# A graph network on one core: transposed edge attributes made where they are used, and two engines' turns put in another order

## The chip, the cores and the metric

The kernel runs on one core of one Trainium2 chip. Its time is device microseconds, from the start of the program to its end. The kernel before took 1757.79 us (median of 3 runs, 1755.62 to 1760.14). A core has a matrix engine (TensorE, PE in the profile; PEld is its weight load), a vector engine (VectorE, DVE), a scalar engine (ScalarE, ACT), GpSimd (POOL) and SyncE (SP), which here only starts transfers. Each works through its own list of instructions in order and waits on semaphores for the others.

## The reference

`x` has 50000 nodes of 128 floats; there are 12500 edges (`src`, `dst`, sorted by `dst`) with attributes of 128 floats. A GraphSAGE part of two layers is followed by a graph transformer of four heads, each with a residual and a layer norm:

```python
x = _layernorm(x + _L0_gnn_ref(x, src, dst, ...))   # two layers: h @ W_self + mean of neighbours @ W_neigh + b
x = _layernorm(x + _L1_gnn_ref(x, edge_index, edge_attr_128, ...))
# inside _L1_gnn_ref, H = 4 heads of D = 128:
q, k, v = x @ Wq + bq, x @ Wk + bk, x @ Wv + bv
e = edge_attr @ We + be
alpha = einsum('ehd,ehd->eh', q[dst], k[src] + e) / sqrt(D)
attn = exp(alpha - amax[dst]) / denom[dst]            # softmax over the edges of one destination
agg = segment_sum((v[src] + e) * attn, dst)
out = agg + x @ Wskip + bskip
lin = (layernorm(out) * ln_g + ln_b) @ Wlin + blin
return elu(lin + x)
```

## The kernel before

Only rows that are the destination of an edge need the graph work. So the program first computes all 50000 rows as if they had no edge, and then does the edges again and scatters the rows that have some over the output. It has five stages with a barrier of all engines between them:

- setup (weights, index rows);
- stage b (`b_*`): all nodes, in 104 turns of 512 rows;
- stage a (`a_*`): first SAGE layer of the edges' rows;
- stage c (`c_*`): second SAGE layer for 12500 edges, in 25 turns of 512 edges (R = 4 tiles of 128). Beside that it reads the edge attributes, transposes them with TensorE (`c_pea`), copies them from PSUM with ScalarE (`c_eT`, line 1123), multiplies them by `We` (line 1108) and stores the product `ve_tab`. It also stores the transposed attributes in `eT_tab` (SyncE, line 1199);
- stage d (`d_*`): attention, layer norms and the scatter of the results, in 111 turns for 98 tiles of 128 edges.

Stage d is a software pipeline. In turn `it` four tiles are in work: `a` = it (gathered rows of source and destination transposed, line 1366; logits), `b` = it - 10 (values and the sum over the edges of one destination), `c` = it - 11 (first layer norm and product with `Wlin`) and `d` = it - 12 (elu, second layer norm, output). Once in 7 tiles a group of logits goes through a softmax by rows: transposed by TensorE, two scans (maxima), then two scans (sums), then a reciprocal, in three successive turns of VectorE. The order of the work on each engine is the order of the code in `d_pe`, `d_act`, `d_dve`, `d_pool` and `d_sync`; nothing reorders it. The steps of one turn that matter here:

- TensorE: 1366 transposes of source and destination rows (`d_pT`), 1373 and 1375 products with `Wv` and `Wskip` for tile b, 1386 with `Aqk` for tile a, 1392 four transposes of tile c (`d_pO`), 1397 with `Aqe` (`d_pP`: the logits' matrix in bank PB is complete), 1402 sum over the edges (`d_pN`), 1408 four products with `Wg` (`d_pY`).
- ScalarE: 1443 copy of the transposes (`d_xT`), 1449 first norm (`d_on`), 1455 exp, 1461 copy of shares (one turn in 7), 1468 values scaled by shares (`d_vex`), 1473 and 1475 the second norm's root (`d_rs2`), 1480 copy of tile c's transposes (`d_onT`), 1494 output (`d_o2`), 1499 and 1501 the first norm's root for tile b (`d_rs`).
- VectorE: 1592 residual (`d_z`), 1596 matrix of equal destinations (`d_same`), 1602 `d_nm`, 1608 values plus attributes (`d_vs`), 1612 and 1616 elu and residual, 1618 and 1622 statistics of the second norm (`d_bn2`), the group's scans (1555 to 1582) in three turns of 7, 1634 `d_nm2`, 1640 four logits (`d_al`), 1646 and 1650 statistics of the first norm (`d_s1`, `d_bn`).
- GpSimd: two gathers (1307), an addition (1320), the scatter of finished rows (1324).
- SyncE: transposed attributes of tile it + 3 read from `eT_tab` (1256), `ve_tab` rows (1260), four small stores of tile c (1266 to 1270).

In the code `after(eng, name, j)` makes the engine wait until step `name` is done for tile `j`.

Of the kernel before, what the change touches and what calls it, by code (L numbers as in the profile page):

```python
# [40 lines left out]
def gnn_kernel(nc, x, src, dst, edge_attr, Ws0, Wn0, b0, Ws1, Wn1, b1, Wq, bq, Wk, bk, Wv, bv, We, be,  # L41
# [21 lines left out]
    eT_tab = nc.dram_tensor("eT_tab", [NT * P, D], F32).ap()  # L63
# [4 lines left out]
    with ExitStack() as ctx:  # L68
# [99 lines left out]
        carve_at[0] = 0  # L168
        d_x1s = [carve(D) for _ in range(4)]
# [104 lines left out]

        def dma_et(k):
            return step(f"dma_et{k}")
# [833 lines left out]
        def c_act(act):  # L1110
            for s in range(NG + 2):
                if s < NG:
                    n = min(R, NT - R * s) * P
                    after(act, "c_pmT", s)
                    after(act, "c_py", s - 2)
                    after(act, "c_col", s - 2)
                    act.activation(c_mnT[s % 2][:, 0:n], MT[s % 2][:, 0:n], ACT.Copy).then_inc(step("c_mnT"), 1)
                    if s == LAST:
                        split_act(act, "c", tile_of(MT[s % 2], NT % R), c_mnT[s % 2][:])
                    after(act, "c_pea", s)  # L1120
                    after(act, "c_pve1", (R * s) // 2 - 1)
                    landed_before(act, dma_et(s % 2), s // 2)
                    act.activation(c_eT[s % 2][:].rearrange("p r d -> p (r d)")[:, 0:n], TE[:, 0:n],
                                   ACT.Copy).then_inc(step("c_eT"), 1)
                if s >= 2:
                    j = s - 2
                    after(act, "c_bn", j)
                    act.activation(a_st[:, 32:36], mv(a_st[:, 24:32])[:, :, 1], ACT.Ln, bias=eps[:, 0:1]).then_inc(step("c_l"), 1)
                    after(act, "c_l", j)
                    after(act, "c_n0", j - 1)  # L1130
                    act.activation(a_st[:, 36:40], a_st[:, 32:36], ACT.Exp, scale=-0.5).then_inc(step("c_r"), 1)
                    after(act, "c_nm", j)
                    landed_before(act, dma_cr[j % 2], j // 2)
                    for r in range(R):
                        t = act.activation(a_rows[j % 2][:, r, :], ypart[:, R * j + r, :], ACT.Identity,
                                           scale=a_st[:, 36 + r:37 + r], bias=a_st[:, 40 + r:41 + r])
                    t.then_inc(step("c_x1"), 1)
                if s < NG:
                    for r in tiles_of(s)[0::2]:
                        attr_out(act, lambda o, i: act.activation(o, i, ACT.Copy), s, r)  # L1140
# [40 lines left out]
        def c_sync(sp):  # L1181
            def load(s):
                after(sp, "c_pea", s - 2)
                if (s + 1) * BLK <= E:
                    sp.dma_start(c_ea[s % 2][:], edge_attr[s * BLK:(s + 1) * BLK, :].rearrange("(r p) d -> p r d", p=P)
# [9 lines left out]
            for s in range(NG + 2):  # L1195
                if s < NG:
                    n = len(tiles_of(s))
                    after(sp, "c_eT", s)
                    sp.dma_start(eT_tab[s * BLK:s * BLK + n * P, :].rearrange("(r p) d -> p r d", p=P),
                                 c_eT[s % 2][:, 0:n, :]).then_inc(dma_et(s % 2), 16)  # L1200
                    if s + 2 < NG:
                        load(s + 2)
# [5 lines left out]
                if s < NG:  # L1208
                    for r in tiles_of(s):
                        i = R * s + r  # L1210
                        after(sp, f"c_ve{r % 2}", i // 2)
                        sp.dma_start(ve_tab[i * P:(i + 1) * P, :], c_ve[i % 4][:]).then_inc(dma_vs(i % 4), 16)
            for k in range(2):
                sp.wait_ge(dma_cr[k], 16 * len(range(k, NG, 2)))
                sp.wait_ge(dma_et(k), 16 * len(range(k, NG, 2)))
# [37 lines left out]
        def d_sync(sp):  # L1253
            def load(j):
                after(sp, "d_pP", j - 4)
                sp.dma_start(d_xT[j % XT][:, 2 * D:3 * D], eT_tab[j * P:(j + 1) * P, :]).then_inc(dma_ea[j % 4], 16)
# [84 lines left out]
        def d_pe(pe):  # L1341
# [12 lines left out]
            for it in range(D_TURNS):  # L1354
# [6 lines left out]
                if live(a):  # L1361
                    pe.wait_ge(dma_xs[a % 4], 16 * (a // 4 + 1))
                    pe.wait_ge(dma_xd[a % 4], 16 * (a // 4 + 1))
                    after(pe, "d_xT", a - 1)
                    for i, s_ in enumerate((d_x1s[a % 4], d_x1d[a % XD])):
# [29 lines left out]
                if live(a):  # L1395
                    pe.wait_ge(dma_ea[a % 4], 16 * (a // 4 + 1))
# [39 lines left out]
        def d_act(act):  # L1436
            for it in range(D_TURNS):
                a, b, c, d = it, it - LAG, it - LAG - 1, it - LAG - 2

                if live(a):  # L1440
                    after(act, "d_pT", a)
                    after(act, "d_pN", a - XT)
                    act.activation(d_xT[a % XT][:, 0:2 * P], TB[:, 0:2 * P], ACT.Copy).then_inc(step("d_xT"), 1)
# [26 lines left out]

                if live(d):
# [4 lines left out]

                if live(c):
                    after(act, "d_pO", c)
                    after(act, "d_pY", c - 1)
                    act.activation(d_onT, OTB[:], ACT.Copy).then_inc(step("d_onT"), 1)  # L1480
# [41 lines left out]
            act.activation(f_out, f_sum, ACT.Identity, scale=f_rs2, bias=f_nm2).then_inc(step("f_out"), 1)  # L1522

        def d_dve(v):
# [59 lines left out]
            for it in range(D_TURNS):  # L1584
# [45 lines left out]

                if live(d):
# [5 lines left out]
                if live(a):  # L1637
                    after(v, "d_pP", a)
                    for h in range(H):
                        t = v.tensor_tensor_reduce(hs(d_junk, h), hs(PB, h), d_x1d[a % XD], SCALE, zero[:, 0:1],  # L1640
                                                   ALU.mult, ALU.add, d_al[:, H * a + h:H * a + h + 1])
# [124 lines left out]
```

## Time and profile before

| | us |
|---|---|
| median of 3 runs | 1757.79 |
| the profiled execution | 1751.26 |
| its span (first to last instruction) | 1749.4 |
| stage b | about 16 to 680 |
| stage a | about 680 to 847 |
| stage c | 847.6 (first load) to 1043 |
| stage d, first turns | 1043 to 1100 |
| stage d, full turns | 1100 to 1640 |
| stage d, last turns and end | 1640 to 1749.4 |

Over 1100 to 1640 us TensorE is busy for 525.3 of 540 us, VectorE for 406.3, ScalarE for 365.1 and GpSimd for 292.1. In stage c (847 to 1043 us, 196 us) they are busy for 153.2, 113.9, 105.3 and 97.9 us, and the DMA engines work at 0.75 of their time. How to read it: a matrix engine that is busy for 97% can still be waited for less than that says, because the ends of matmuls are modelled and a matmul row covers time in which the next one has already begun. What sets the length of a turn is read from a timeline: go from an instruction back to what it started right behind, until the same instruction of the turn before is reached. In each row of the timeline the first number is the start, the second the duration, and a bracket at the end says how long the engine had been idle and for whom.

### The profile page before, as it was taken

Reading aid. Unit: us, or ns where it says so; the run is one execution under the profiler, and the core shown is the slowest. Engines: PE = TensorE matmul, PEld = TensorE weight load, DVE = VectorE, ACT = ScalarE, POOL = GpSimd, SP = SyncE. Lnnn points to the kernel's source line nnn. Section 1 sums busy time; section 2 is a strip of 40 time slices with the busy share of each in tenths; the row PEclk is TensorE's granted clock in tenths of the full one; section 3 lists DMA queues with packets and bytes.
Section 4 is the critical chain, followed back from the end, with each engine's and each line's share of the span. In section 5 each row is a group of like instructions: output and inputs, shape, how many; then the busy total and the mean of one; then the engine's idle time right before and its main releaser. Section 6 shows DMA issues by size and latency. Waiting matters only on the chain. (4 is left out here: it accounts for less than half of the span.)

```text
span 1749.4 us, 34139 instructions
## 1 busy us (share of the span) xinstructions
PE 1524.3 (87%) x7745; PEld 1024.5 (59%) x7745; DVE 1327.1 (76%) x6197; ACT 1160.0 (66%) x3125; POOL 1041.2 (60%) x1038
## 2 busy tenths in 40 slices
PE   3599999999999998999688867999999999999872
PEld 2477777777777776777455543555555555455441
DVE  4799999999999996656366653777777777777762
ACT  0499999999999995333255541666666666666662
POOL 4688888868888773664455526455555555555320
PEclk9899999999999999999899988999999999999995
DMA  2356566544444442332388853233222232333210
GB/s 79 109 152 158 153 160 154 151 154 144 149 142 148 139 146 74 85 84 70 116 268 271 273 173 80 78 84 85 83 84 84 84 85 79 82 83 85 59 36 4
DMA packets 178820, 206.77 MB, mean 118 GB/s; under 512 B 36607, under 2 KB 104666, under 8 KB 178703
## 3 DMA queue, kind: packets, MB, share of 16 engines
q1 hardware_dynamic: 151502, 169.25, 31.5%
q0 software_dynamic: 27200, 36.26, 9.0%
q8 instruction: 37, 0.61, 0.2%
q14 instruction: 81, 0.66, 0.1%
HBM read 107.47 MB, written 106.49 MB: 122 GB/s over the span
## 5 line engine op out<-in xcount | busy, mean ns | idle before, releaser
L1307 POOL DMA_INDIRECT big<-x_tab,look x196 | 199.6, 1019 | 97.6 <-issue 56.1
L1324 POOL DMA_INDIRECT out_dram<-big,idx x98 | 99.2, 1013 | 259.1 <-DVE big L1640 126.3
L700 PE MATMUL pb<-MG_s,big 128*128 128x256 f32 x832 | 207.4, 392 | 41.5 <-issue 30.7
L700 PEld LDWEIGHTS pb<-MG_s,big 128*128 128x128 f32 x832 | 149.5, 189 | 143.7 <-issue 95.2
L725 ACT ACTIVATE big<-big 128x128 f32<-128x128 f32 x416 | 170.0, 481 | 0.0
L820 POOL TENSOR_TENSOR big<-big,cl 128x512 f32<-128x512 f32 x104 | 133.3, 1282 | 49.8 <-ACT big L749 40.5
L682 PE MATMUL pb<-C_s,big 128*128 128x128 f32 x832 | 161.6, 276 | 0.0
L683 PE MATMUL pb<-Ws1c_s,big 128*128 128x128 f32 x832 | 161.3, 276 | 0.0
L1057 POOL DMA_INDIRECT big<-h1e_tab,hidx x98 | 97.9, 999 | 103.9 <-PE pb L937 45.0
L334 POOL DMA_INDIRECT a_xs<-in_x_dram,idx x98 | 102.3, 1044 | 86.7 <-issue 47.6
L1408 PEld LDWEIGHTS pb<-Wg_s,big 128*128 128x128 f32 x784 | 95.8, 192 | 98.1 <-ACT big L1480 95.8
L860 POOL DMA_INDIRECT look<-redirect,idx x98 | 118.4, 1208 | 29.5 <-issue 29.2
L1640 DVE CUSTOM_DVE_ANT_0 big<-pb,big,zero 128x128 f32<-128x128 f32 x392 | 113.2, 342 | 28.2 <-PE pb L1397 25.9
L834 POOL DMA_INDIRECT redirect<-idx x98 | 112.3, 1146 | 30.9 <-issue 30.6
L1408 PE MATMUL pb<-Wg_s,big 128*128 128x128 f32 x784 | 114.2, 289 | 18.9 <-ACT big L1480 15.7
L683 PEld LDWEIGHTS pb<-Ws1c_s,big 128*128 128x128 f32 x832 | 126.9, 193 | 0.0
L682 PEld LDWEIGHTS pb<-C_s,big 128*128 128x128 f32 x832 | 126.9, 193 | 0.0
L749 ACT ACTIVATE big<-pb,big 128x128 f32<-128x128 f32 x416 | 118.9, 369 | 11.9
L716 ACT ACTIVATE big<-pb,vcol 128x512 f32<-128x512 f32 x104 | 71.5, 688 | 78.1 <-issue 59.1
L762 DVE CUSTOM_DVE_ANT_0 big<-pb,big,zero 128x128 f32<-128x128 f32 x416 | 120.5, 345 | 1.9 <-ACTq L256 1.9
L1108 PE MATMUL pb<-We_s,a_xs 128*128 128x512 f32 x196 | 99.3, 632 | 22.7 <-issue 19.0
L799 DVE SCALAR_TENSOR_TENSOR big<-pb,big 128x128 f32<-128x128 f32 x416 | 116.7, 343 | 1.4 <-issue 1.4
(345 smaller groups left out, 4015.1 us busy)
## 6 DMA issues: line engine op xcount, KB each, us to landing
big<-in_x_dram SPq DMA_DIRECT2D x104, 256.0 KB
x_tab<-big SPq DMA_DIRECT2D x98, 256.0 KB
out_dram<-big SPq DMA_DIRECT2D x98, 256.0 KB
ve_tab<-c_ve SPq DMA_DIRECT2D x98, 256.0 KB
c_ve<-ve_tab SPq DMA_DIRECT2D x98, 256.0 KB
h1e_tab<-a_rows SPq DMA_DIRECT2D x25, 256.0 KB
x_tab<-a_rows SPq DMA_DIRECT2D x25, 256.0 KB
big<-eT_tab SPq DMA_DIRECT2D x98, 64.0 KB
```

The lines of the kernel that those rows point to most:

```text
L682: pe.matmul(o, b_xT[(u - 1) % 2][:, r * P:(r + 1) * P], C_s[:], start=True, stop=False)
L683: t = pe.matmul(o, b_h1T[:, r * P:(r + 1) * P], Ws1c_s[:], start=False, stop=True)
L700: t = pe.matmul(o, b_x1T[:, r * P:(r + 1) * P], MG_s[:], start=True, stop=True)
L725: t = act.activation(b_o[u % 2][:, r * D:(r + 1) * D], b_w[u % 2][:, r * D:(r + 1) * D], ACT.Identity, scale=brs3[:, r:r + 1], bias=b_nm3[ ...
L749: t = act.activation(b_x1[(u - 1) % 4][:, r * D:(r + 1) * D], PY[(u - 1) % 2][:, r * D:(r + 1) * D], ACT.Copy, bias=1.0, scale=brs1[:, r:r ...
L762: t = v.tensor_tensor_reduce(b_junk[:, r * D:(r + 1) * D], PMG[(u - 3) % 2][r // 2][:, (r % 2) * 256 + 128:(r % 2) * 256 + 256], b_x1[(u - ...
L799: t = v.scalar_tensor_tensor(out=b_z[(u - 3) % 2][:, r * D:(r + 1) * D], in0=PMG[(u - 3) % 2][r // 2][:, (r % 2) * 256:(r % 2) * 256 + 128 ...
L820: g.tensor_tensor(b_x1c[u % 2].rearrange("p (r d) -> p r d", r=R), b_x1[(u - 2) % 4].rearrange("p (r d) -> p r d", r=R), cl[:].rearrange(" ...
L860: g.indirect_dma_start(out=look[:, 0, e:e + 1], out_offset=None, in_=redirect, in_offset=bass.IndirectOffsetOnAxis(ap=idx[:, SRC, e:e + 1] ...
L1307: g.indirect_dma_start(out=o, out_offset=None, in_=x1_tab, in_offset=bass.IndirectOffsetOnAxis(ap=look[:, a, j:j + 1], axis=0), bounds_che ...
L1408: t = pe.matmul(LY, hs(d_onT, h), Wg_s[:, h, :], start=(h == 0), stop=(h == H - 1))
L1640: t = v.tensor_tensor_reduce(hs(d_junk, h), hs(PB, h), d_x1d[a % XD], SCALE, zero[:, 0:1], ALU.mult, ALU.add, d_al[:, H * a + h:H * a + h ...
```

## The change

Three things. (1) `eT_tab` goes: stage c no longer stores the transposed attributes, and stage d reads the attributes as they are into `d_ea` and transposes them with TensorE as a third transpose beside the two of line 1366; the copy of line 1443 covers 384 columns in place of 256. TensorE now waits for the attributes at the head of its turn and no longer before line 1397. (2) In stage c a partition reads four successive rows of the attributes (2 KB) in place of four rows that lie 128 apart (512 B each), and `ve_tab` is stored so that its rows come to the same place. (3) In stage d ScalarE's `d_onT` copy stands ahead of the root `d_ln2`, `d_rs2`, and VectorE makes two of the four logits ahead of `d_nm2` and two behind it.

```diff
-    eT_tab = nc.dram_tensor("eT_tab", [NT * P, D], F32).ap()
+        d_ea = [carve(D) for _ in range(4)]
@@ stage c, ScalarE
-                    landed_before(act, dma_et(s % 2), s // 2)
@@ stage c, SyncE
-                    sp.dma_start(c_ea[s % 2][:], edge_attr[s * BLK:(s + 1) * BLK, :].rearrange("(r p) d -> p r d", p=P)
+                    sp.dma_start(c_ea[s % 2][:], edge_attr[s * BLK:(s + 1) * BLK, :].rearrange("(p r) d -> p r d", r=R)
...
-                if s < NG:
-                    n = len(tiles_of(s))
-                    after(sp, "c_eT", s)
-                    sp.dma_start(eT_tab[s * BLK:s * BLK + n * P, :].rearrange("(r p) d -> p r d", p=P),
-                                 c_eT[s % 2][:, 0:n, :]).then_inc(dma_et(s % 2), 16)
-                    if s + 2 < NG:
-                        load(s + 2)
+                if s + 2 < NG:
+                    load(s + 2)
...
-                        sp.dma_start(ve_tab[i * P:(i + 1) * P, :], c_ve[i % 4][:]).then_inc(dma_vs(i % 4), 16)
+                        if (s + 1) * BLK <= E:
+                            place = ve_tab[s * BLK:(s + 1) * BLK, :].rearrange("(p r) d -> p r d", r=R)[:, r, :]
+                        else:
+                            place = ve_tab[i * P:(i + 1) * P, :]
+                        sp.dma_start(place, c_ve[i % 4][:]).then_inc(dma_vs(i % 4), 16)
@@ stage d, SyncE
-                after(sp, "d_pP", j - 4)
-                sp.dma_start(d_xT[j % XT][:, 2 * D:3 * D], eT_tab[j * P:(j + 1) * P, :]).then_inc(dma_ea[j % 4], 16)
+                after(sp, "d_pT", j - 4)
+                n = min(P, E - j * P)
+                sp.dma_start(d_ea[j % 4][0:n, :], edge_attr[j * P:j * P + n, :]).then_inc(dma_ea[j % 4], 16)
@@ stage d, TensorE
+                    pe.wait_ge(dma_ea[a % 4], 16 * (a // 4 + 1))
                     after(pe, "d_xT", a - 1)
-                    for i, s_ in enumerate((d_x1s[a % 4], d_x1d[a % XD])):
+                    for i, s_ in enumerate((d_x1s[a % 4], d_x1d[a % XD], d_ea[a % 4])):
                         t = pe.transpose(TB[:, i * P:(i + 1) * P], s_, ident[:])
...
-                    pe.wait_ge(dma_ea[a % 4], 16 * (a // 4 + 1))
@@ stage d, ScalarE (d_onT of tile c now stands ahead of d_ln2 and d_rs2 of tile d)
-                    act.activation(d_xT[a % XT][:, 0:2 * P], TB[:, 0:2 * P], ACT.Copy).then_inc(step("d_xT"), 1)
+                    act.activation(d_xT[a % XT], TB[:, 0:3 * P], ACT.Copy).then_inc(step("d_xT"), 1)
@@ stage d, VectorE
+                if live(a):
+                    after(v, "d_pP", a)
+                    for h in range(H // 2):
+                        logits(v, a, h)
+
                 if live(d):
                     after(v, "d_rs2", d)
                     ...
                 if live(a):
-                    after(v, "d_pP", a)
-                    for h in range(H):
+                    for h in range(H // 2, H):
```

Line numbers shift by 1 to 7 with the change. On ScalarE, in stage d, the rows from the root of the first norm (1499) to the copy `d_onT` (1480) of a turn without a group stand like this before:

```order
903 L1499 ACTIVATE big<-big,eps 128x1
904 L1501 ACTIVATE big<-big 128x1
905 L1443 ACTIVATE big<-pb 128x256
906 L1449 ACTIVATE big<-pb,big 128x512
907 L1455 ACTIVATE big<-big,neg 128x128
908 L1468 ACTIVATE big<-pb,big 128x128 x4
909 L1473 ACTIVATE big<-big,eps 128x1
910 L1475 ACTIVATE big<-big 128x1
911 L1480 ACTIVATE big<-pb 128x512
```

The same place on ScalarE after the change, where L1469 is the copy `d_onT`:

```order
903 L1494 ACTIVATE big<-big,eps 128x1
904 L1496 ACTIVATE big<-big 128x1
905 L1438 ACTIVATE big<-pb 128x384
906 L1444 ACTIVATE big<-pb,big 128x512
907 L1450 ACTIVATE big<-big,neg 128x128
908 L1463 ACTIVATE big<-pb,big 128x128 x4
909 L1469 ACTIVATE big<-pb 128x512
910 L1473 ACTIVATE big<-big,eps 128x1
911 L1475 ACTIVATE big<-big 128x1
```

The copy of 512 columns moved ahead of the two small ones, and the first copy grew to 384 columns. On VectorE, stage d, the rows from `d_bn2` (1622) to `d_bn` (1650) of such a turn before (the pairs of L1640 are one logit each, the product and the read of its sum):

```order
1561 L1622 BN_AGGR big<-big 128x2
1562 L1634 SCALAR_TENSOR_TENSOR big<-big 128x1
1563 L1640 ISA big<-pb,big,zero 128x128
1564 L1640 ISA big 128x1
1565 L1640 ISA big<-pb,big,zero 128x128
1566 L1640 ISA big 128x1
1567 L1640 ISA big<-pb,big,zero 128x128
1568 L1640 ISA big 128x1
1569 L1640 ISA big<-pb,big,zero 128x128
1570 L1640 ISA big 128x1
1571 L1646 BN_STATS big<-pb 128x6
1572 L1650 BN_AGGR big<-big 128x2
```

And the same place on VectorE after the change, where L1520 is the new helper `logits` and L1638 is `d_nm2`:

```order
1561 L1621 BN_AGGR big<-big 128x2
1562 L1520 ISA big<-pb,big,zero 128x128
1563 L1520 ISA big 128x1
1564 L1520 ISA big<-pb,big,zero 128x128
1565 L1520 ISA big 128x1
1566 L1638 SCALAR_TENSOR_TENSOR big<-big 128x1
1567 L1520 ISA big<-pb,big,zero 128x128
1568 L1520 ISA big 128x1
1569 L1520 ISA big<-pb,big,zero 128x128
1570 L1520 ISA big 128x1
1571 L1648 BN_STATS big<-pb 128x6
1572 L1652 BN_AGGR big<-big 128x2
```

Two logits moved ahead of `d_nm2`; in a turn with a group's scans these stand behind `d_bn2` and ahead of all four logits, as before. On TensorE the row of two transposes per turn becomes one of three, at the same place.

## Rows read from the trace of the kernel before

**Rows 1.** Stage c: busy PE, PEld, DVE, ACT, POOL; clock, DMA share, GB/s.
```profile
920.00:960.00 40.00, 34.00 (x163) 21.17 (x161) 27.02 (x114) 24.60 (x59) 22.75 (x23) 1.00 0.85 273
```

**Rows 2.** Timeline, one turn of stage c: start, duration, engine, line.
```profile
945.25 0.57 ACT L1140 ACTIVATE c_ve<-pb 128x512 f32<-128x512 f32 x1
...
945.88 1.98 PE L1108 MATMUL pb<-We_s,a_xs 128*128 128x512 f32 x4 [1.00 <-issue]
...
952.91 1.99 PE L1108 MATMUL pb<-We_s,a_xs 128*128 128x512 f32 x4 [1.00 <-issue]
```

**Rows 3.** Timeline, one turn of stage d without a group's work.
```profile
1194.08 0.38 PE L1366 MATMUL pb<-ident,big 128*128 128x128 f32 x2
1194.24 1.01 POOL L1324 DMA_INDIRECT out_dram<-big,idx  x1 [2.01 <-DVE big L1640]
...
1194.56 0.18 DVE L1650 BATCH_NORM_AGGREGATE big<-big 128x2 f32<-128x6 f32 x1
...
1194.98 0.32 DVE L1596 TENSOR_SCALAR big<-dst_row,dst_f 128x128 f32<-128x128 uint16 x1
...
1195.21 0.37 ACT L1443 ACTIVATE big<-pb 128x256 f32<-128x256 f32 x1
...
1196.51 1.13 ACT L1468 ACTIVATE big<-pb,big 128x128 f32<-128x128 f32 x4
1196.64 0.29 DVE L1612 SCALAR_TENSOR_TENSOR big<-big 128x128 f32<-128x128 f32 x1 [0.52 <-issue]
1196.87 0.60 PE L1392 MATMUL pb<-ident,big 128*128 128x128 f32 x4
...
1197.31 1.02 PE L1397 MATMUL pb<-Aqe_s,big 128*128 128x512 f32 x2
...
1197.95 0.18 DVE L1622 BATCH_NORM_AGGREGATE big<-big 128x2 f32<-128x6 f32 x1 [0.37 <-DVE big L1618]
...
1198.17 1.02 PE L1402 MATMUL pb<-big 128*128 128x512 f32 x2
...
1198.60 0.58 ACT L1480 ACTIVATE big<-pb 128x512 f32<-128x512 f32 x1
1198.72 0.16 DVE L1634 SCALAR_TENSOR_TENSOR big<-big 128x1 f32<-128x1 f32 x1 [0.59 <-ACT big L1475]
1198.80 0.35 DVE L1640 CUSTOM_DVE_ANT_0 big<-pb,big,zero 128x128 f32<-128x128 f32 x1
...
1199.23 1.16 PE L1408 MATMUL pb<-Wg_s,big 128*128 128x128 f32 x8
...
1199.88 0.70 DVE L1646 BATCH_NORM_STATS2 big<-pb 128x6 f32<-128x512 f32 x1
1200.23 0.38 PE L1366 MATMUL pb<-ident,big 128*128 128x128 f32 x2
...
1200.71 0.18 DVE L1650 BATCH_NORM_AGGREGATE big<-big 128x2 f32<-128x6 f32 x1
```

**Rows 4.** Timeline of VectorE in a turn with two of a group's scans.
```profile
1204.10 0.18 DVE L1622 BATCH_NORM_AGGREGATE big<-big 128x2 f32<-128x6 f32 x1 [0.37 <-DVE big L1618]
...
1205.30 0.14 DVE L1634 SCALAR_TENSOR_TENSOR big<-big 128x1 f32<-128x1 f32 x1
```

**Rows 5.** Timeline of TensorE: the transpose once in 7 turns, twice in succession.
```profile
1353.37 0.24 PE L1360 MATMUL pb<-ident,big 28*128 28x28 f32 x1
...
1397.58 0.24 PE L1360 MATMUL pb<-ident,big 28*128 28x28 f32 x1
```

**Rows 6.** Timeline, the last turns of stage d, with no new tile.
```profile
1676.24 1.00 POOL L1324 DMA_INDIRECT out_dram<-big,idx  x1 [4.43 <-ACT big L1494]
...
1676.53 0.76 DVE L1596 TENSOR_SCALAR big<-dst_row,dst_f 128x128 f32<-128x128 uint16 x1
...
1679.59 1.10 PE L1402 MATMUL pb<-big 128*128 128x512 f32 x2 [0.76 <-ACT big L1468]
...
1681.04 0.97 PEld L1408 LDWEIGHTS pb<-Wg_s,big 128*128 128x128 f32 x8 [1.18 <-ACT big L1480]
```

More of the change, by code:

```diff
@@ L273, in dma_ce @@
             return step(f"dma_ce{k}")
-        def dma_et(k):
-            return step(f"dma_et{k}")
         def dma_vs(k):
@@ L1211, in c_sync @@
                         after(sp, f"c_ve{r % 2}", i // 2)
-                        sp.dma_start(ve_tab[i * P:(i + 1) * P, :], c_ve[i % 4][:]).then_inc(dma_vs(i % 4), 16)
+                        if (s + 1) * BLK <= E:
[3 more added lines that the diff above has]
+                        sp.dma_start(place, c_ve[i % 4][:]).then_inc(dma_vs(i % 4), 16)
             for k in range(2):
                 sp.wait_ge(dma_cr[k], 16 * len(range(k, NG, 2)))
-                sp.wait_ge(dma_et(k), 16 * len(range(k, NG, 2)))
             for k in range(4):
@@ L1469, in d_act @@
                     t.then_inc(step("d_vex"), 1)
+                if live(c):
+                    after(act, "d_pO", c)
+                    after(act, "d_pY", c - 1)
+                    act.activation(d_onT, OTB[:], ACT.Copy).then_inc(step("d_onT"), 1)
                 if live(d):
@@ L1475, in d_act @@
                     act.activation(d_rs2, d_lw2, ACT.Exp, scale=-0.5).then_inc(step("d_rs2"), 1)
[L1477 to L1480, printed above, removed]
                 if ends_group(a - 1):
@@ L1522, in d_act, with logits @@
             act.activation(f_out, f_sum, ACT.Identity, scale=f_rs2, bias=f_nm2).then_inc(step("f_out"), 1)
+        def logits(v, a, h):
+            return v.tensor_tensor_reduce(hs(d_junk, h), hs(PB, h), d_x1d[a % XD], SCALE, zero[:, 0:1],
+                                          ALU.mult, ALU.add, d_al[:, H * a + h:H * a + h + 1])
         def d_dve(v):
@@ L1637, in d_dve @@
                 if live(a):
-                    after(v, "d_pP", a)
-                    for h in range(H):
-                        t = v.tensor_tensor_reduce(hs(d_junk, h), hs(PB, h), d_x1d[a % XD], SCALE, zero[:, 0:1],
-                                                   ALU.mult, ALU.add, d_al[:, H * a + h:H * a + h + 1])
+                    for h in range(H // 2, H):
+                        t = logits(v, a, h)
                     t.then_inc(step("d_al"), 1)
```

## The prediction

> **What bounds the kernel now.** I read the windows by stage first, then timelines of one turn of each stage that the change touches, walking back from an instruction to what it started right behind until the same instruction of the turn before came up. The share of busy time would mislead here: in stage d TensorE is busy for 525.3 of 540 us (the table of the profile), and still the full turn is not set by it.
>
> Stage d, a turn without a group's scans [rows 3]. VectorE's `d_bn` (1650) starts at 1194.56 and again at 1200.71: 6.15 us. Between the two the work goes round one loop of VectorE and ScalarE: from `d_bn` over ScalarE's root, `d_nm`, the norm `d_on` and exp to the elu (1612) at 1196.64, 2.08 us; to `d_bn2` (1622) at 1197.95, 1.31; over the second root on ScalarE (VectorE is idle for 0.59) to `d_nm2` (1634) at 1198.72, 0.77; to the first logit at 1198.80, 0.08; four logits to `d_s1` (1646) at 1199.88, 1.08; to `d_bn`, 0.83. The sum is 6.15, so nothing else is in the loop. TensorE follows with slack: line 1402 starts at 1198.17, and at the pace of the matmul before it (1197.31 to 1198.17, 0.86) line 1408 could start at 1199.03. It starts at 1199.23, behind ScalarE's copy of line 1480 (1198.60 and 0.58 long): 0.20 lost. Having waited costs more: 1408 to the next 1366 takes 1.00, where eight halves at 0.11 make 0.88. TensorE needs 6.15 - 0.20 - 0.12 = 5.83 us per turn.
>
> In three turns of seven a group's scans stand between `d_bn2` and `d_nm2`: 1.20 us in place of 0.77 [rows 4], so the loop is 6.15 + 0.43 = 6.58. Seven turns take 1397.58 - 1353.37 = 44.21 [rows 5], which is 4 x 6.15 + 3 x 6.54.
>
> In the last turns, with no new tile, line 1402 starts at 1679.59 and line 1408 only at 1681.04, behind the same ScalarE copy [rows 6].
>
> Stage c: line 1108's third tile starts at 945.88, right behind the end of ScalarE's copy at 945.25 + 0.57, and again at 952.91 [rows 2]: 7.03 us, and 20 of the stage's turns take 7.03 or 7.04. The DMA engines are at 0.85 [rows 1], but a turn paced by transfers would not repeat to 0.01 us, and the engine that releases it is ScalarE, in order through its own copies.
>
> **The change, part by part.**
>
> *No store of transposed attributes, 25 times 256 KB, in stage c.* SyncE's issue slots and the transfers are beside a chain of ScalarE and TensorE [rows 2]; in its place in the chain stands nothing. The wait on the store's landing ahead of the copy `c_eT` goes; the store was issued two turns before, 14 us. I take 0. The other end: if transfers paced the turn, one eighth of the bytes (256 of 2048 KB: attributes 256, transposed 256, rows 256, gathers 256, `ve_tab` 1024) would go, 25 x 7.03 / 8 = 22 us. Above zero I see no price: there are fewer bytes.
>
> *Attributes by 2 KB a partition, `ve_tab` rows 8 KB apart.* As many bytes, fewer pieces to read, the same 2 KB pieces to write. 0, under the cover of the same 7.03 us; ends within the 22 us above.
>
> *Third transpose on TensorE, 98 times.* Four transposes take 0.60 and two take 0.38 [rows 3], so one more costs (0.60 - 0.38) / 2 = 0.11: 5.83 + 0.11 = 5.94 per turn. The upper end is its whole duration of some 0.27 (0.38 less 0.11).
> The page "TensorE: Matmul & The Clock Gate" of the Trainium skill, Part 4 (PE-mode transpose), gives some 275 ns for a 128x128 transpose in a kernel, and so speaks against trading a transfer for one. The spacing in the trace contradicts it as a cost per piece, though 0.27 agrees as the length of one alone; by the page's figure TensorE's turn would be 6.11, and the estimate for the kernel that of the first rival below.
>
> *Wait for the attributes at TensorE's head rather than ahead of 1397.* Behind it stand all products of the turn. Their load is issued three turns ahead, now after `d_pT` in place of `d_pP`, and in SyncE's queue it stands behind the same four small stores; three turns are 18 us. 0.
>
> *Wider copy on ScalarE.* 256 columns take 0.37, 512 take 0.58 [rows 3]: 384 take 0.47, 0.10 to 0.11 more. It stands between the first root and `d_on`, so up to 0.11 enters the loop; less where `d_nm` is the later.
>
> *The copy `d_onT` ahead of the second root.* The scaled values (1468) end at 1196.51 + 1.13 = 1197.64 and the four transposes at 1197.47, so the copy can run from 1197.64 to 1198.22. It then is off TensorE's path, which asks for it at 1199.03: the 0.20 and 0.12 are gone. The root now starts at about 1198.16; behind the copy it starts at 1198.2. Nothing is late.
>
> *Two logits ahead of `d_nm2`.* They fill the 0.59 in which VectorE idles. From `d_bn2` to `d_s1` now 1.93; then no sooner than the root allows, 0.77 + 0.08 + two logits 0.54 = 1.39: the loop loses 0.54. New loop: 6.15 - 0.54 + at most 0.11 = 5.72. What is late next is TensorE with 5.94. A turn goes from 6.15 to 5.94, 0.21 less.
> In a turn with scans there is no idle time to fill: the same instructions stand between `d_bn2` and `d_s1`, in another order. 6.54 stays, with up to 0.11 more for the wider copy, and less by what the loop has in hand over TensorE after four short turns (0.2 to 0.3, at most once for each of the three). Seven turns: 4 x 5.94 + 3 x 6.54 = 43.4, 0.8 less; ends 0.5 (0.11 more each) and 1.5 (0.25 in hand each). I take 0.9, since what is in hand surely counts once. From the 12th tile to the 98th there are 87 turns, 12.4 times seven: -11 us (-6 to -18.6).
>
> *Last 13 turns.* Line 1408 could start 0.86 behind 1402, at 1680.45 in place of 1681.04 [rows 6]: 0.59 at most, 7.7 in all; the VectorE loop there still holds the root. I take 0.4 over 12 turns: -5 (0 to -7.7).
>
> *First 11 turns.* They hang on one logit bank (1386, 1397, four logits, next 1386), in which nothing changes: 0.
>
> *GpSimd's scatter and `d_same`.* Now `d_same` (1596) starts 0.74 after the scatter (1324) and takes 0.32 [rows 3]. Where it starts 0.29 after it, it takes 0.76 and ends 1.05 after the scatter's start [rows 6]. After the change `d_bn` comes 0.25 sooner and the scatter's release, `d_o2` behind `d_nm2`, 0.1 later, so it starts some 0.4 after the scatter: into that hold. `d_nm` is then about 0.1 late, hidden in short turns (5.72 against 5.94) and not in those with scans: 3 x 0.1 x 12.4 = 3; I charge +2 (0 to +6).
> The page "SBUF — State Buffer" of the Trainium skill (section on the two separate sides) says that VectorE and GpSimd share one port pair, locked for a whole instruction, the loser fully blocked. The 0.76 agrees with it; the third rival below is its case, priced from rows.
>
> Sum: -11 - 5 + 2 = -14 us. The profiled execution took 1751.26, so 1737; it ran 6.5 us below the median of the runs shown, 1757.79, and by that 1744.
>
> **Rivals.**
>
> First, TensorE's turn is dearer than 5.94: the third transpose costs its 0.27, or the copy waits. Then 6.11, a short turn gains 0.04, seven gain about 0.2 or 0.3, in all -3 - 5 + 2 = -6: 1751. For it: nothing in the trace shows three in a row. Against: four and two differ by exactly 0.11 each.
>
> Second, stage c was paced by transfers: 22 us more, 1722. For it: the share of 0.85. Against: 7.03 every time, and the release by ScalarE [rows 2].
>
> Third, slower: the scatter holds `d_same` in every turn of stage d. If `d_same` starts with the scatter, it ends 1.05 after it, 0.7 later than now, and pushes `d_nm` by about 0.6. The loop is 5.72 + 0.6 = 6.32 (+0.17), with scans 7.29 (+0.75): 2.9 per seven, 36 in all, and nothing from the last turns: 1794. It decides from the point where `d_nm` is pushed by over 0.2, since 4 x 5.94 + 3 x 6.89 = 44.4 is today's 44.21. For it: the move of 0.35 towards the scatter and the 0.76 of the last turns. Against: it comes to 0.1 by my count, and the last turns live with it at 5.9.
>
> Fourth, no change to speak of, 1756: a loop that I did not see is as long as the present one.
>
> **How the numbers follow.** Forecast 0.70, first rival 0.12, second 0.06, third 0.08, fourth 0.04. What a measurement of this kernel can tell from no change is about 0.3%, 5 us. The forecast's own range is -26 to 0, 1732 to 1758. Faster: 0.95 of the forecast, 0.6 of the first rival and the second, 0.67 + 0.07 + 0.06 = 0.80; slower the third, 0.08; the rest, 0.12, is within. The range of 8 in 10 is 1731 to 1758: the forecast, the first and the fourth; the second and the third stay out.
>
> **What would show it.** In the profile after: stage c still 7.03 us a turn with a lower DMA share; transposes in threes with 0.11 between them; short turns of 5.95, with TensorE not idle ahead of 1408; turns with scans at 6.4 to 6.6; VectorE without a wait for the root in turns of either kind; `d_same` at 0.7 us often. Wrong: short turns of 6.1 or more, or a stage c of another length.

## The result, and the profile after

Four executions of the changed kernel have a median of 1739.46 us (1738.74 to 1740.18), four of the kernel before 1756.84 (1755.62 to 1760.14). The ratio is 0.9898, with a 95% interval of 0.9881 to 0.9915: faster by 1.0%. The forecast was 1744.

The spans of the two profiled executions, cut at starts of instructions (stage c from the first to the last of ScalarE's copies `c_mnT`, the "middle turns" from the 12th tile's transposes to the 98th's, the last turns from there to the start of the last tile's product `d_pY`, line 1408 before and 1403 after):

| us | before | after | difference | forecast |
|---|---|---|---|---|
| before stage c | 856.7 | 859.5 | +2.8 | 0 |
| stage c | 169.0 | 169.2 | +0.2 | 0 |
| first 11 turns of stage d | 44.0 | 44.5 | +0.5 | 0 |
| middle turns | 547.4 | 536.9 | -10.5 | -11, and +2 for the scatter |
| last turns | 71.9 | 68.1 | -3.8 | -5 |
| span | 1749.4 | 1738.4 | -11.0 | -14 |

(What is left between the rows and the span is the step into stage d and the end of the program, -0.2 together.) The first row is none of the change's: no instruction ahead of stage c differs. The profiled execution before, 1751.26, lay 5.6 below its median, that of after, 1740.18, 0.7 above its own; so the spans differ by less than the medians do (11.0 against 17.4). The middle and the last turns together give -14.3.

Stage c, the window that answers to [rows 1]: busy PE, PEld, DVE, ACT, POOL; clock, DMA share, GB/s.

```profile
923.00:963.00 40.00, 33.99 (x163) 21.16 (x162) 26.98 (x114) 24.61 (x59) 22.68 (x23) 1.00 0.75 235
```

The turn that answers to [rows 2], from its timeline:

```profile
945.92 1.98 PE L1105 MATMUL pb<-We_s,a_xs 128*128 128x512 f32 x4
...
952.95 1.98 PE L1105 MATMUL pb<-We_s,a_xs 128*128 128x512 f32 x4
```

The DMA share fell from 0.85 to 0.75 and the turn is still 952.95 - 945.92 = 7.03 us: about an eighth of the transfers went (235 GB/s in place of 273) and nobody had waited for them.

A short turn of stage d, which answers to [rows 3]:

```profile
1359.35 0.49 PE L1362 MATMUL pb<-ident,big 128*128 128x128 f32 x3
1359.76 0.18 DVE L1652 BATCH_NORM_AGGREGATE big<-big 128x2 f32<-128x6 f32 x1
1359.83 1.01 POOL L1319 DMA_INDIRECT out_dram<-big,idx  x1 [1.59 <-PE pb L1362]
1360.17 0.28 DVE L1595 TENSOR_SCALAR big<-dst_row,dst_f 128x128 f32<-128x128 uint16 x1
1360.41 0.47 ACT L1438 ACTIVATE big<-pb 128x384 f32<-128x384 f32 x1
...
1361.87 0.29 DVE L1611 SCALAR_TENSOR_TENSOR big<-big 128x128 f32<-128x128 f32 x1 [0.43 <-ACT big L1450]
...
1362.69 1.02 PE L1392 MATMUL pb<-Aqe_s,big 128*128 128x512 f32 x2
1362.89 0.60 ACT L1469 ACTIVATE big<-pb 128x512 f32<-128x512 f32 x1
1363.18 0.18 DVE L1621 BATCH_NORM_AGGREGATE big<-big 128x2 f32<-128x6 f32 x1 [0.37 <-DVE big L1617]
...
1363.55 1.02 PE L1397 MATMUL pb<-big 128*128 128x512 f32 x2
1363.75 0.35 DVE L1520 CUSTOM_DVE_ANT_0 big<-pb,big,zero 128x128 f32<-128x128 f32 x1 [0.39 <-issue]
1364.30 0.15 DVE L1638 SCALAR_TENSOR_TENSOR big<-big 128x1 f32<-128x1 f32 x1
1364.41 1.05 PE L1403 MATMUL pb<-Wg_s,big 128*128 128x128 f32 x8
1364.91 0.69 DVE L1648 BATCH_NORM_STATS2 big<-pb 128x6 f32<-128x512 f32 x1
1365.30 0.49 PE L1362 MATMUL pb<-ident,big 128*128 128x128 f32 x3
```

The turn is 1365.30 - 1359.35 = 5.95 us, from 6.15. TensorE's last three steps now follow each other without a gap: 1392 to 1397 0.86, 1397 to 1403 0.86 (it was 1.06 before), 1403 to the next 1362 0.89 (it was 1.00). The three transposes take 0.49, where two took 0.38. ScalarE's `d_onT` (1469) ends at 1363.49, long before 1403 asks for it. On VectorE `d_nm2` (1638) no longer waits for ScalarE; the one wait left in the stretch, 0.39 ahead of the first logit, ends 0.20 after TensorE's 1397 begins, so it is for the product `d_pP` of 1392. The bound has moved from the VectorE-ScalarE loop to TensorE.

The once-in-seven-turns transpose, which answers to [rows 5]:

```profile
1309.34 0.24 PE L1355 MATMUL pb<-ident,big 28*128 28x28 f32 x1
...
1352.67 0.24 PE L1355 MATMUL pb<-ident,big 28*128 28x28 f32 x1
```

43.33 us in place of 44.21. The seven turns are 5.95 three times, 6.06, and 6.26, 6.64, 6.51 for those with scans. The 6.06 is the turn in which TensorE also transposes the group's logits (line 1378), which takes it 0.11.

The last turns, which answer to [rows 6]:

```profile
1659.68 1.10 PE L1397 MATMUL pb<-big 128*128 128x512 f32 x2 [0.98 <-ACT big L1463]
1660.61 1.05 PE L1403 MATMUL pb<-Wg_s,big 128*128 128x128 f32 x8
```

1403 now follows 1397 by 0.93 and waits for nobody; before it came 1.45 later. The end of these turns is disturbed by TensorE's clock, in either kernel:

```profile
1711.92 2.08 PE L1408 MATMUL pb<-Wg_s,big 128*128 128x128 f32 x8 [2.21 <-ACT big L1480]
```

```profile
1690.20 1.91 PE L1403 MATMUL pb<-Wg_s,big 128*128 128x128 f32 x8
```

The first is the last product before, the second the last but two after; in most of these turns the same product takes 1.16 before and 1.05 after. The granted clock was 0.50 from 1709.8 us in the profile of before and from 1689.3 to 1692.7 in that of after, the level of 1.2 GHz, and 1.00 (2.4 GHz) ahead of that. The first nine of these turns, all at 2.4 GHz, take 52.8 before and 49.7 after, 3.1 less.

### The profile page after: what moved, and what is told of

The parts are those of the page before. It is cut to its first block and busy times, and to the rows that moved or that the text cites. A ratio compares the mean times of both kernels' runs of the same rounds, so it can differ in the third digit from the quotient of the medians.

```text
span 1738.4 us, 34404 instructions
## 1 busy us (share of the span) xinstructions
PE 1523.6 (88%) x7843; PEld 1044.6 (60%) x7843; DVE 1327.5 (76%) x6197; ACT 1173.1 (67%) x3125; POOL 1035.8 (60%) x1038
## 5 line engine op out<-in xcount | busy, mean ns | idle before, releaser
L1520 DVE CUSTOM_DVE_ANT_0 big<-pb,big,zero 128x128 f32<-128x128 f32 x392 | 118.9, 341 | 40.2 <-PE pb L1392 29.4
L1403 PEld LDWEIGHTS pb<-Wg_s,big 128*128 128x128 f32 x784 | 103.6, 193 | 47.9 <-issue 37.6
L1382 PE MATMUL pb<-Aqk_s,big 128*128 128x512 f32 x196 | 106.4, 625 | 18.5 <-DVE big L1520 7.8
L759 DVE CUSTOM_DVE_ANT_0 big<-pb,big,zero 128x128 f32<-128x128 f32 x416 | 120.2, 343 | 2.0 <-ACTq L256 1.9
```

Of the source, the lines that this page charges most:

```text
L759: t = v.tensor_tensor_reduce(b_junk[:, r * D:(r + 1) * D], PMG[(u - 3) % 2][r // 2][:, (r % 2) * 256 + 128:(r % 2) * 256 + 256], b_x1[(u - ...
L1520: return v.tensor_tensor_reduce(hs(d_junk, h), hs(PB, h), d_x1d[a % XD], SCALE, zero[:, 0:1], ALU.mult, ALU.add, d_al[:, H * a + h:H * a + ...
```

## The experiments

The theory under test: a short turn is the longer of two things, a loop of VectorE and ScalarE and TensorE's own sequence; stage c has room for the transfers; so all the gain comes from the two reorderings, together, and the third transpose takes back 0.11 a turn. The rivals: the gain comes from fewer transfers or from one reordering alone, or the transpose costs its full length. Ratios are to the kernel before, timed on the same chip, with 95% intervals. Chips differ by more than 1% (the kernel before takes 1727 us on some and 1752 to 1757 on others), so times of different chips are not set against each other; the undisturbed turns of stage d are, since they repeat across chips (the changed stage d, seven turns: 43.33 in the first trace, 43.31 in the second, 43.34 in the run with the doubled store).

**Only the reordering.** The kernel before, with `d_onT` ahead of the root and two logits ahead of `d_nm2`; the transposed table is stored and read as before.

```diff
+                if live(c):
+                    after(act, "d_pO", c)
+                    after(act, "d_pY", c - 1)
+                    act.activation(d_onT, OTB[:], ACT.Copy).then_inc(step("d_onT"), 1)
                 if live(d):
                     after(act, "d_bn2", d)
...
+                if live(a):
+                    after(v, "d_pP", a)
+                    for h in range(H // 2):
...
-                    for h in range(H):
+                    for h in range(H // 2, H):
```

> The kernel before with the third part of the change alone (copy d_onT ahead of the root, two logits ahead of d_nm2); the transposed attributes are still stored and read. Theory of two loops (VectorE-ScalarE loop 6.15 us before, TensorE 5.84 without its waits): short turns of stage d 5.84, turns with scans 6.0 to 6.55, stage c 7.03 a turn, so 5 to 7 us faster than the changed kernel: about 1733 us. Rival, the store in stage c or the load from eT_tab was what cost: stage c and d then stay as before and it takes about 1750 us or more.

Measured: 1703.5 us against 1727.18, ratio 0.9862 (0.9847 to 0.9877). A short turn, from TensorE's timeline:

```profile
1327.94 0.38 PE L1366 MATMUL pb<-ident,big 128*128 128x128 f32 x2
...
1333.78 0.38 PE L1366 MATMUL pb<-ident,big 128*128 128x128 f32 x2
```

5.84, where the prediction put TensorE's need at 5.83. The turns with scans are 6.26, 6.63 and 6.53, those of the changed kernel. Half of the change does better than the whole: 0.9862 against 0.9898, and the two intervals do not overlap (one ends at 0.9877, the other begins at 0.9881). Seven turns are 42.91 here and 43.33 in the changed kernel, about four times the 0.11 of a transpose.

**Only the attributes' part.** The changed kernel with both reorderings undone.

```diff
-                    act.activation(d_onT, OTB[:], ACT.Copy).then_inc(step("d_onT"), 1)
                 if live(d):
...
+                    act.activation(d_onT, OTB[:], ACT.Copy).then_inc(step("d_onT"), 1)
...
-                    for h in range(H // 2):
-                        logits(v, a, h)
```

> The changed kernel with both engines' order as before; the attributes are transposed in stage d and not stored. Theory of two loops: the loop through the wider copy is 6.17 to 6.2, TensorE 5.95 is hidden: short turns 6.17, whole kernel +2 to +6 us over the kernel before, 1759 to 1763 us. Rival, the store in stage c paced that stage or disturbed it: faster than before by 5 us or more.

Measured: ratio 1.0021 (1.0012 to 1.003). From VectorE's timeline, and the product that stands behind `d_onT`:

```profile
1344.04 0.18 DVE L1648 BATCH_NORM_AGGREGATE big<-big 128x2 f32<-128x6 f32 x1
...
1348.75 1.16 PE L1403 MATMUL pb<-Wg_s,big 128*128 128x128 f32 x8
...
1350.24 0.18 DVE L1648 BATCH_NORM_AGGREGATE big<-big 128x2 f32<-128x6 f32 x1
```

The short turn is 6.20 here and 6.19 on average, 0.04 over the kernel before: TensorE's 5.95 is hidden under the loop, and of the wider copy's 0.10 some 0.04 enters it. Leaving the table out brings nothing: stage c, first to last `c_mnT`, is 168.4 long here and 168.4 in the run with only the reordering, which has the store, on the same chip. The rest of that part costs a fifth of a per cent.

**One reordering alone, twice.** First the changed kernel with all four logits in one piece behind `d_nm2` (`d_onT` stays ahead of the root):

```diff
-                    for h in range(H // 2):
-                        logits(v, a, h)
...
-                    for h in range(H // 2, H):
+                    after(v, "d_pP", a)
+                    for h in range(H):
```

> The changed kernel with its four logits in one piece behind d_nm2 again; the copy d_onT stays ahead of the root. Theory of two loops: the loop still has the root and four logits in it, 6.17 to 6.2 a short turn; only the last 13 turns gain (some 4 to 5 us): 1755 to 1758 us. Rival, TensorE's wait for the copy was the bound (0.3 us a turn): this one edit gives nearly all of the gain, 1740 to 1744 us.

Measured: ratio 1.0003 (0.9994 to 1.0012). From its timeline:

```profile
1350.92 0.18 DVE L1621 BATCH_NORM_AGGREGATE big<-big 128x2 f32<-128x6 f32 x1 [0.37 <-DVE big L1617]
1350.93 1.02 PE L1397 MATMUL pb<-big 128*128 128x512 f32 x2
1351.70 0.16 DVE L1633 SCALAR_TENSOR_TENSOR big<-big 128x1 f32<-128x1 f32 x1 [0.60 <-ACT big L1475]
1351.79 1.05 PE L1403 MATMUL pb<-Wg_s,big 128*128 128x128 f32 x8
```

TensorE's gap ahead of 1403 is closed (0.86 after 1397, not 1.06), yet the turn is 6.2: VectorE still stands 0.60 for the root, and the loop sets the end. What TensorE saved it waits elsewhere. Only the last turns gain: 69.9, against 72.4 in the run with only the attributes' part on the same chip (each with a stretch at the lower clock near its end).

Then the other one, the two logits ahead of `d_nm2`, with `d_onT` behind the root:

```diff
-                if live(c):
-                    ...
-                    act.activation(d_onT, OTB[:], ACT.Copy).then_inc(step("d_onT"), 1)
                 if live(d):
                     ...
+                if live(c):
+                    ...
+                    act.activation(d_onT, OTB[:], ACT.Copy).then_inc(step("d_onT"), 1)
```

> The changed kernel with the copy d_onT behind the root again; the logits stay two and two. Theory of two loops: the VectorE-ScalarE loop falls to 5.7, and TensorE waits a little for the copy in some turns: short turns 5.95 to 6.1, last 13 turns as before, 1744 to 1750 us. Rival, TensorE's wait for the copy was the bound: no gain over the kernel before, 1757 us or more.

Measured: ratio 0.9964 (0.9951 to 0.9978). From TensorE's and ScalarE's timeline of two successive turns:

```profile
1345.69 1.02 PE L1397 MATMUL pb<-big 128*128 128x512 f32 x2
1346.00 0.58 ACT L1475 ACTIVATE big<-pb 128x512 f32<-128x512 f32 x1
1346.63 1.16 PE L1403 MATMUL pb<-Wg_s,big 128*128 128x128 f32 x8
...
1351.83 1.02 PE L1397 MATMUL pb<-big 128*128 128x512 f32 x2
1352.69 1.06 PE L1403 MATMUL pb<-Wg_s,big 128*128 128x128 f32 x8
```

The loop is broken, and now TensorE waits for `d_onT` in every second turn (0.94 from 1397 to 1403, then 0.86), with turns of 5.95 and 6.15 in alternation, the longer ones just over the 6.1 that I expected. Seven undisturbed turns, each with the third transpose: 44.42 with neither reordering, 44.49 with the copy alone, 43.90 with the split alone, 43.33 with both. The two are worth more together (1.09) than the sum of each alone (0.45): each removes one of two limits that lie 0.2 from each other.

**The changed kernel again,** beside the next one on the same chip, no edit.

> The changed kernel itself, to stand beside the others on one chip. Both theories: 0.99 of the kernel before; short turns 5.95.

Measured: 1733.76 us against 1752.17, ratio 0.9899 (0.9883 to 0.9915), the result once more.

**A fourth transpose,** which writes one more tile that no one reads.

```diff
-                    for i, s_ in enumerate((d_x1s[a % 4], d_x1d[a % XD], d_ea[a % 4])):
+                    for i, s_ in enumerate((d_x1s[a % 4], d_x1d[a % XD], d_ea[a % 4], d_ea[a % 4])):
```

> The changed kernel with the transpose of the attributes made twice (a fourth transpose into unused columns of the same bank), 98 more. Theory TensorE is the bound after the change: short turns 6.06 (+0.11), turns with scans longer by 0 to 0.05, 4 to 8 us over the changed kernel, ratio to before about 0.993. Rival, VectorE and ScalarE still set the turn (5.95 by chance): no change, 0.990.

Measured: 1739.8 us, ratio 0.9931 (0.9913 to 0.9949).

```profile
1364.08 0.60 PE L1362 MATMUL pb<-ident,big 128*128 128x128 f32 x4
...
1370.14 0.60 PE L1362 MATMUL pb<-ident,big 128*128 128x128 f32 x4
```

A short turn is 6.06: 0.11 for one more transpose, and 5.84, 5.95, 6.06 for two, three, four. That each is felt in full shows TensorE as the bound of a short turn after the change, and 0.11 as its price. "TensorE: Matmul & The Clock Gate" of the Trainium skill, Part 4 (PE-mode transpose), gives some 275 ns for one in a kernel. That is near the 0.27 that one alone is long here, but it is not the price of one more in a row, which these runs have at 0.11.

**Twice the store of `ve_tab`.** A second store of the same tile to another table, 256 KB for each of the stage's tiles: 1 MB more a turn of stage c.

```diff
+    ve_twice = nc.dram_tensor("ve_twice", [NT * P, HC], F32).ap()
...
                         sp.dma_start(place, c_ve[i % 4][:]).then_inc(dma_vs(i % 4), 16)
+                        sp.dma_start(ve_twice[i * P:(i + 1) * P, :], c_ve[i % 4][:]).then_inc(dma_vs(i % 4), 16)
```

> The changed kernel with each tile of ve_tab stored twice in stage c (once more into a table that nobody reads): 2.8 MB a turn in place of 1.8. Theory, stage c is paced by ScalarE and TensorE and has DMA time in hand: with a share of about 0.8 now, 1.5 times as much no longer fits, so a turn grows from 7.03 to 8.5 to 9.5 us, and it is seen how much more the removed store (0.26 MB) would have needed before it cost something. Rival, transfers are not paced by bytes at all: 7.03 stays.

Measured: 1722.64 us, ratio 0.9969 (0.9958 to 0.998), 0.7% over the changed kernel's ratio. The window over most of the stage (same columns as above):

```profile
863.00:1023.00 160.00, 131.27 (x588) 79.32 (x587) 95.73 (x397) 88.41 (x210) 77.98 (x78) 0.98 1.01 351
```

Here the transfers do set the pace: a share of 1.01 and 351 GB/s, turns of 7.04 at first, then 7.5, and up to 10.0; the stage is 181.0 long, where it is 168.4 in the next run, on the same chip. On average a turn is 7.54; my expectation of 8.5 to 9.5 was too high. The changed kernel moves 235 GB/s in this stage and the kernel before 273 [rows 1], both well below 351; so 256 KB less a turn was worth nothing.

**`d_same` later.** To see what GpSimd's scatter does to VectorE's `d_same`, I put it behind `d_nm`.

```diff
-                if live(b):
-                    after(v, "d_pN", b - 2)
-                    v.tensor_scalar(d_same[b % 2], ...
                 if live(c):
...
+                if live(b):
+                    after(v, "d_pN", b - 2)
+                    v.tensor_scalar(d_same[b % 2], ...
```

> The changed kernel with d_same behind d_nm in VectorE's turn, so that it starts some 0.65 us after GpSimd's scatter in place of 0.33. Theory of the hold (VectorE's tensor_scalar is held where it overlaps 0.4 to 0.8 us after the scatter's start): d_same takes 0.39 to 0.45 in place of 0.28, d_vs starts 0.15 to 0.2 later, and since TensorE sets the short turns at 5.95 the kernel changes by 0 to 4 us. Rival, the 0.32 and 0.76 of the kernel before had another cause: d_same stays at 0.28.

Measured: ratio 0.9904 (0.9887 to 0.992), the same as the changed kernel.

```profile
1330.58 1.01 POOL L1319 DMA_INDIRECT out_dram<-big,idx  x1 [1.59 <-PE pb L1362]
1331.36 0.28 DVE L1601 TENSOR_SCALAR big<-dst_row,dst_f 128x128 f32<-128x128 uint16 x1
```

It starts 0.78 after the scatter, not the 0.65 that I expected, and takes 0.28, not 0.39 to 0.45. So the run shows that neither place costs anything, but it does not test a start at 0.65.

**The scans moved into a wait.** With the two reorderings the turns with scans (6.26 to 6.64) are the long ones. Each of the three scan steps is cut in two, and its first half (the first scan of the maxima, of the sums, the reciprocal of the shares) put right behind `d_vs`, where VectorE waits for ScalarE's exp (the 0.43 ahead of line 1611 in the short turn above). TensorE's transpose of the logits, which the maxima need, comes up right behind the turn's first transposes.

```diff
+                if ends_group(a - 1):
+                    maxima_ahead((a - 1) // GT, rows_in((a - 1) // GT))
+                if ends_group(a - 2):
+                    sums_ahead((a - 2) // GT, rows_in((a - 2) // GT))
+                if ends_group(a - 3):
+                    shares_ahead((a - 3) // GT, rows_in((a - 3) // GT))
+
                 if live(d):
                     after(v, "d_e", d)
```

On the changed kernel:

> The changed kernel with a group's scans shared between two places of VectorE's turn: first scan of maxima, first scan of sums and the reciprocal right behind d_vs, where VectorE waits 0.5 us for the exp; the rest behind d_bn2 as before. Theory two loops: the three turns with scans fall from 6.26, 6.64 and 6.51 to between 6.05 and 6.3, 0.7 to 1.2 us per seven turns, 8 to 14 us less than the changed kernel. Rival, what lengthens these turns is TensorE's extra transposes or the exp on ScalarE: no gain, or a loss of some us since the elu comes later.

Measured: 1718.6 us, ratio 0.9811 (0.9794 to 0.9828). VectorE in a turn with the reciprocal, in the changed kernel and then in this one:

```profile
1350.82 0.18 DVE L1621 BATCH_NORM_AGGREGATE big<-big 128x2 f32<-128x6 f32 x1 [0.37 <-DVE big L1617]
1350.92 0.91 DVE L1575 RECIPROCAL big<-big 28x128 f32<-28x128 f32 x1
...
1352.07 0.33 DVE L1520 CUSTOM_DVE_ANT_0 big<-pb,big,zero 128x128 f32<-128x128 f32 x1
```

```profile
1337.04 0.93 DVE L1582 RECIPROCAL big<-big 28x128 f32<-28x128 f32 x1
1337.90 0.22 DVE L1628 SCALAR_TENSOR_TENSOR big<-big 128x128 f32<-128x128 f32 x1
...
1339.14 0.18 DVE L1638 BATCH_NORM_AGGREGATE big<-big 128x2 f32<-128x6 f32 x1 [0.37 <-DVE big L1634]
1339.56 0.33 DVE L1521 CUSTOM_DVE_ANT_0 big<-pb,big,zero 128x128 f32<-128x128 f32 x1
```

From `d_bn2` to the first logit it is 0.42 in place of 1.25; the reciprocal's 0.86 stand ahead of the elu instead, partly in its wait. The turns with scans are 5.95, 6.22 and 6.01 in place of 6.26, 6.64 and 6.51, and seven turns take 42.09 in place of 43.33. The gain over the changed kernel on the same chip, 1733.76 - 1718.6 = 15 us, is a little over the 8 to 14 that I expected. The earlier transpose of the logits was not tried apart from the rest.

And on the kernel before with only the reorderings, which gives the best version of the study:

> The kernel before (attributes transposed in stage c and stored) with the two orders changed and the scans in two places. Theory two loops: short turns 5.84, turns with scans 6.0 to 6.25: faster than all others, ratio to before 0.978 to 0.982. Rival, TensorE no longer counts once the scans are apart: the same time as the changed kernel with the scans apart.

Measured: 1710.35 us, ratio 0.9767 (0.9745 to 0.9788), faster than either kernel and just past the 0.978 that I expected at best; seven turns 41.33, the short ones 5.84.

## Why the prediction was right

*Two limits, 6.15 and 5.83, and the loop as the longer.* Right to 0.01 us. The reordering alone brought 5.84; adding the third transpose to it gave 5.95 (forecast 5.94); undoing the reorderings alone gave 6.19. No third loop of the old length exists, so the fourth rival falls.

*No store, 2 KB pieces, wait at TensorE's head: 0.* Right. Stage c kept 7.03 with the share down from 0.85 to 0.75, and the doubled store showed where transfers begin to pace it. The second rival (1722) falls. The 2 KB pieces were not tried apart from the rest; with the table's removal they add up to no time in stage c.

*Third transpose 0.11.* Right, shown by the runs with two, three and four. The first rival (1751) falls.

*Wider copy, up to 0.11.* The copy takes 0.47 as forecast. In the loop it is felt with 0.04 where the loop bounds (6.19 against 6.15), and not at all behind the reordering: turns with scans are 6.26, 6.63, 6.53 with the narrow and 6.26, 6.64, 6.51 with the wide one.

*The reorderings: 0.21 a short turn, nothing in one with scans but what is in hand.* 0.20 a short turn and, in seven turns, 43.33 where 43.3 was taken. Inside the seven it was a little different: 6.26, 6.64 and 6.51 rather than three of 6.54, so what the loop has in hand goes mostly into the first turn with scans. The short turn ahead of them took 6.06, not 5.94: TensorE has the group's transpose in it (line 1378, 0.11), which the prediction left out. Middle turns -10.5, forecast -11.

*Last 13 turns.* -3.8, forecast -5 (0 to -7.7). The mechanism is right (1403 no longer waits), the size was taken somewhat too high: the first nine turns, at full clock, gain 0.35 each, not 0.4, and the last three only 0.7 together, with a stretch of 3.4 us at 1.2 GHz in them after the change.

*First 11 turns 0.* +0.5, where both profiles have long waits and 10 us at 1.2 GHz in these turns (see the last section). At full clock these turns took 37.4 with two transposes and 37.7 with three (the first four experiments, one chip), so the third transpose is felt there too, with 0.3.

*Scatter against `d_same`, +2.* The one term whose mechanism was wrong. The start was forecast well: some 0.4 after the scatter, and it is 1360.17 - 1359.83 = 0.34. What failed is the duration: 0.28 in nearly every turn, not 0.7. `d_same` was long in ten turns of the changed kernel only, and the start alone does not say which. Three pairs of scatter and `d_same`: one of the kernel before in a full turn, then two of the changed kernel, in a full turn and in one without new gathers:

```profile
1499.47 1.01 POOL L1324 DMA_INDIRECT out_dram<-big,idx  x1 [0.17 <-issue]
...
1499.95 0.28 DVE L1596 TENSOR_SCALAR big<-dst_row,dst_f 128x128 f32<-128x128 uint16 x1
```

```profile
1134.85 1.01 POOL L1319 DMA_INDIRECT out_dram<-big,idx  x1 [2.53 <-ACT big L1489]
...
1135.39 0.52 DVE L1595 TENSOR_SCALAR big<-dst_row,dst_f 128x128 f32<-128x128 uint16 x1
...
1621.80 1.01 POOL L1319 DMA_INDIRECT out_dram<-big,idx  x1 [1.39 <-ACT big L1489]
...
1622.14 0.72 DVE L1595 TENSOR_SCALAR big<-dst_row,dst_f 128x128 f32<-128x128 uint16 x1
```

So the third rival (1794) falls as well. I had one row at 0.29 [rows 6], from turns without gathers, and took it for a rule in all turns. In the full turns of the changed kernel `d_same` starts 0.33 to 0.36 after the scatter more than 70 times and is never held; from the turn at 1622 on, starts at 0.34 (0.72 and 0.71), 0.38 and 0.47 are. What in the scatter differs between the two kinds of turn stays open. Without the term the sum is -16, and the ratio of 0.9898 is -17.9 on 1756.84, with an interval of -14.9 to -20.9. By the profiled execution's own time the forecast was 1737 and that of after took 1740.18; most of that difference is the +2.8 ahead of stage c, where nothing was changed. That the two stretches priced at -14 gave -14.3 is partly luck: the scatter's +2 did not come, and the gain was 0.5 short in the middle turns and 1.2 short in the last.

What stays open: both kernels have two turns of 7.5 to 7.8 us in the middle, in which the scatter comes 3.3 us after its release `d_o2` rather than 0.83. I did not find what holds it, and both have it alike. All four traces of the chip where the kernel before takes 1752 us have two such turns as well, while the six traces of the chips where it takes 1727 us have none over 7.1 us in the middle.

## What to carry over

Where two engines' limits lie near each other, walk each limit out to the hundredth from one turn's timeline and price an edit by what is left when the other becomes the longer: here, in seven turns, one reordering alone brought nothing, the other 0.5, and both together 1.1. A transfer that no one waits for was worth nothing to remove, even at a share of 0.85, and the work put in its place on the engine that became the bound was paid in full in the short turns. After such a step, look in the turns that did not get shorter for work (here scans) that can stand in another engine's wait.

## What the runs showed of the hardware

- *Held VectorE.* `d_same` is 0.28 long alone. In full turns it is 0.28 too when it starts 0.33 to 0.47 after the scatter's start, and longer when it starts between 0.53 and 0.74 (at 0.53 0.52, at 0.58 0.48, at 0.70 0.37, at 0.74 0.32); at 0.78 it is 0.28 again. In turns without gathers it is held from 0.28 on (0.76 in the kernel before; 0.71 and 0.72 at 0.34, 0.66 or 0.87 at 0.38, 0.57 at 0.47, 0.43 at 0.62), with one exception in the kernel before (0.28 at 0.28). All that are held here but the 0.87 end about 1.05 after the scatter's start. "SBUF — State Buffer" of the Trainium skill, section "SBUF: two separate sides", has the pair of engines' lock held for a whole instruction. These rows agree with that for the end of the hold; its beginning moves, and over 70 instructions that ran wholly within the scatter's 1.0 us were not held.
- *Price of having waited.* 1403 to the next transposes takes 0.89 when 1403 comes straight behind 1397, and 1.00 when it waited before.
- *Ceiling of transfers.* 351 GB/s at a share of 1.01, for stage c's mix of loads, gathers and stores.
- *Waits and clock at the start of stage d.* The first 11 turns took 41.8 to 44.5 us in some profiled executions and 37.4 to 37.7 in others. It goes with the chip and not with the kernel: all six traces of the slower chips (the kernel before at 1752 to 1757 us) are of the first kind, all six of the chips where it takes 1727 us of the second. The changed kernel's code there was 44.5 long once and 41.8 the second time. In the first kind two or three of the early turns, elsewhere 3.3 each, take 4 to 8.5, and the granted clock falls among them; but the clock cannot be all of it. In the run with four transposes, whose first 11 turns took 44.0, it was at the lower level for 3.4 us, which by an estimate costs 1.7 at most, while ScalarE's copy came 4.15 after the end of the transposes that it reads and TensorE stood for 4.69 behind it, before the clock fell at 1062.4:

```profile
1056.70 0.60 PE L1362 MATMUL pb<-ident,big 128*128 128x128 f32 x4
...
1061.45 0.49 ACT L1438 ACTIVATE big<-pb 128x384 f32<-128x384 f32 x1 [6.62 <-remote]
```

What held the copy is open. Windows over 38 us from the stage's start, with the clock as the third number from the end, of the changed kernel and then of the one with only the reordering:

```profile
1051.00:1089.00 38.00, 26.52 (x74) 12.00 (x72) 14.14 (x79) 5.21 (x11) 22.84 (x24) 0.87 0.26 76
```

```profile
1032.00:1070.00 38.00, 27.36 (x81) 12.23 (x80) 18.53 (x103) 5.83 (x17) 27.94 (x30) 1.00 0.35 94
```

A granted clock of 0.87 as a mean holds some 10 us at the lower level of 1.2 GHz; in the other run all of it is at 2.4 GHz. TensorE had idled for 11.5 us in the step into the stage in both. The two kinds lie some 6 us apart, which no edit made, a third of the change's whole gain, and it is why the stages' lengths are compared turn by turn above and times only as ratios of runs on one chip.
